# Two weight buffers in place of three, and one-hot tiles with two picks innermost

## What is computed

```
h = tok(x)                                   # embeddings, 3 graph vectors, projection, layernorm
h = h + conv(layernorm(h))                   # causal convolution along the sequence, generated filter
h = h + ffn(layernorm(h))                    # mixture of experts, 8 experts, top 2

def ffn(x):                                  # 8192 rows of 192
    logits = x @ Wr.T                        # (rows, 8)
    vals, idx = top_k(logits, 2)
    share = softmax(vals)
    e_out[e] = gelu(x @ Wi[e].T + bi[e]) @ Wo[e].T + bo[e]    # 192 -> 768 -> 192
    return sum_k share[k] * e_out[idx[k]]
```

## Time and profile before

| | |
|---|---|
| median of 3 runs | 1200.1 us (1199.15 to 1202.99) |
| the profiled execution | 1199.93 us, span 1198.0 us, mean granted clock of TensorE 0.784 |
| busy: PE, PEld, DVE | 955.7 (80%), 907.0 (76%), 615.1 us (51%) |
| busy: ACT, POOL | 518.6 (43%), 670.7 us (56%) |
| DMA | 146.96 MB, 123 GB/s in the mean |
| the costliest groups | L883 and L884 ACT gelu 212.4 and 214.6 us; L510 POOL scatter 236.6; L730 to L732 PE down 211.6, 209.9, 209.7; L711 to L715 PE up 116.6 each |

### The profile page before, as it was taken

How to read it: one execution, slowest core, us unless ns; L and a number is a source line. 1 busy time by engine, 2 the same in 40 slices (tenths; PEclk the granted TensorE clock), 3 DMA queues, 4 the chain that set the end, 5 groups by cost and what they waited for, 6 DMA issues and landing times. The chain is left out here.

```text
span 1198.0 us, 22895 instructions
## 1 busy us (share of the span) xinstructions
PE 955.7 (80%) x7666; PEld 907.0 (76%) x7666; DVE 615.1 (51%) x2089; ACT 518.6 (43%) x1211; POOL 670.7 (56%) x592
## 2 busy tenths in 40 slices
PE   1678677768677687594977699999988998999991
PEld 0578677778677687594964399999978998999981
DVE  2035343445444456538957356665544654665551
ACT  1002121311212123355755376767655665767660
POOL 6455564646565640003520268867767777888774
PEclk9975665656665666795555599999999999999996
DMA  6315261616162533581098174485486465434342
GB/s 208 106 53 176 81 209 53 217 50 214 46 222 94 170 110 114 167 241 53 1 256 263 28 199 62 61 224 129 86 218 151 60 141 120 61 61 61 61 51 30
DMA packets 101114, 146.96 MB, mean 123 GB/s; under 512 B 13476, under 2 KB 81223, under 8 KB 98983
## 3 DMA queue, kind: packets, MB, share of 16 engines
q0 software_dynamic: 39552, 53.26, 23.0%
q1 hardware_dynamic: 60470, 82.26, 21.8%
q10 hardware_dynamic: 1008, 10.34, 2.4%
HBM read 107.00 MB, written 38.82 MB: 122 GB/s over the span
## 5 line engine op out<-in xcount | busy, mean ns | idle before, releaser
L883 ACT ACTIVATE Hs<-bank,U 128x256 bf16<-128x256 f32 x426 | 212.4, 498 | 182.6 <-PE bank L715 153.8
L474 POOL DMA_INDIRECT ev_g<-in_word_emb,ids_i x192 | 192.9, 1004 | 166.1 <-PE bank L573 111.9
L510 POOL DMA_INDIRECT out<-Hs,id_s x142 | 236.6, 1666 | 85.4 <-issue 83.3
L1204 DVE TENSOR_TENSOR Hs<-Hs 128x512 bf16<-128x512 f32 x213 | 147.5, 692 | 146.6 <-ACT Hs L884 131.3
L884 ACT ACTIVATE Hs<-bank,U 128x256 f32<-128x256 f32 x426 | 214.6, 504 | 0.0
L730 PE MATMUL bank<-U,Hs 128*128 128x192 bf16 x852 | 211.6, 248 | 0.2 <-issue 0.2
L732 PE MATMUL bank<-U,Hs 128*128 128x192 bf16 x852 | 209.9, 246 | 0.0
L731 PE MATMUL bank<-U,Hs 128*128 128x192 bf16 x852 | 209.7, 246 | 0.0
L501 POOL DMA_INDIRECT blob<-xtab_d,id_g x142 | 144.2, 1015 | 111.7 <-DVEq L1188 61.1
L573 PE MATMUL bank<-cs,ev_g 128*128 128x1 f32 x384 | 97.8, 318 | 42.6 <-issue 42.6
L572 PE MATMUL bank<-cs,ev_g 128*128 128x1 f32 x384 | 96.1, 314 | 39.4 <-issue 39.3
(11 more groups left out here) (183 smaller groups left out, 1735.2 us busy)
## 6 DMA issues: line engine op xcount, KB each, us to landing
U<-blob_d SPq DMA_DIRECT2D x20, 771.0 KB
U<-blob_d SPq DMA_DIRECT2D x20, 672.0 KB
adj_s<-in_adj SPq DMA_DIRECT2D x48, 256.0 KB
ev_g<-kpad_d SPq DMA_DIRECT2D x24, 512.0 KB, 5.3
wst<-in_wsrc SPq DMA_DIRECT2D x8, 1344.0 KB
blob_d<-blob ACTq DMA_DIRECT2D x7, 1443.0 KB
xtab_d<-U SPq DMA_DIRECT2D x4, 1552.0 KB, 8.8
out<-Hs SPq DMA_DIRECT2D x4, 1536.0 KB, 11.5
```

What stands on the lines that cost most here:

```text
L474: pool.indirect_dma_start(ev_g[:, p, j, b, :], None, t["word_emb"], bass.IndirectOffsetOnAxis(ap=ids_i[:, 1 + j, i * Q + b:i * Q + b + 1], ...
L510: pool.indirect_dma_start(out, bass.IndirectOffsetOnAxis(ap=id_s[:, 2 * q + h:2 * q + h + 1], axis=0), yo[:, q % RX, h, :], None, compute_ ...
L883: f(hh[w][:, d, :], ps, ACT.Gelu, bias=bi[:, d:d + 1])
L1204: last = v.tensor_tensor(hl[w][:, c:c + 2, :], hf[w][:, c:c + 2, :], hh[w][:, c:c + 2, :], ALU.subtract)
```

## The change

The weights get WB = 2 buffers, so even tiles use one and odd tiles the other; the other buffers stay at three. The one-hot tiles are laid out `(a m n i)`, with i = 2 picks innermost and m = 4 pairs outside the columns: PE reads a plane with a step of 2 elements, ACT's half of a tile is contiguous, and `iota_r` holds each number twice and is read four times over.

```diff
 W3 = 3
-ROUNDS = -(-NT // W3)
+WB = 2
+ROUNDS = -(-NT // WB)
...
-        iota_r = sb("iota_r", [128, NC, PICKS], bf16)
+        iota_r = sb("iota_r", [128, NC, 2], bf16)
...
-        hot_p = wst[:, 0:1024].bitcast(bf16).rearrange("p (a n i) -> p a n i", a=2, i=PICKS)
+        hot_p = wst[:, 0:1024].bitcast(bf16).rearrange("p (a m n i) -> p a m n i", a=2, m=PICKS // 2, i=2)
...
-        wbuf = [U_room[:, w * BLOB:(w + 1) * BLOB] for w in range(W3)]
+        wbuf = [U_room[:, w * BLOB:(w + 1) * BLOB] for w in range(WB)]
...
             def reload(it):
-                for w in range(W3):
-                    q = W3 * it + w
+                for w in range(WB):
+                    q = WB * it + w
                     if isinstance(q, int) and q >= NT:
                         break
-                    e, held = expert(q), expert(q - W3)
-                    sp.wait_ge(gelu, FC // 2 * (q - W3 + 1))
+                    e, held = expert(q), expert(q - WB)
+                    sp.wait_ge(gelu, FC // 2 * (q - WB + 1))
...
-                    sp.wait_ge(biased, q - W3 + 1)
+                    sp.wait_ge(biased, q - WB + 1)
...
-                    last = mm(sums(i % TB), hot_p[:, g % 2, :, i], hot_s[:, g % 2, :, i], start=False, stop=False)
+                    last = mm(sums(i % TB), hot_p[:, g % 2, i // 2, :, i % 2], hot_s[:, g % 2, i // 2, :, i % 2], start=False, stop=False)
...
             def up_tile(q):
-                it, w = q // W3, q % W3
+                it, w = q // WB, q % WB
...
-                x0, x1, x2 = (xgT[:, w, c, :] for c in range(3))
+                x0, x1, x2 = (xgT[:, q % W3, c, :] for c in range(3))
...
-                    i = slice(k * TB, (k + 1) * TB)
-                    last = f(hot_s[:, g % 2, :, i], hot_q[:, g % 2, :, i], ACT.Copy, scale=powers[:, k, g:g + 1])
+                    m = slice(k * TB // 2, (k + 1) * TB // 2)
+                    last = f(hot_s[:, g % 2, m, :, :], hot_q[:, g % 2, m, :, :], ACT.Copy, scale=powers[:, k, g:g + 1])
...
-                here = places[:, g, :, :].rearrange("p k t -> p (k t)")
-                return v.tensor_tensor(out, iota_r[:, 0:width, :], repeat(here, 1, width), ALU.is_equal)
+                here = places[:, g, :, :].rearrange("p k (m i) -> p (k m) i", i=2)
+                return v.tensor_tensor(out, repeat(iota_r[:, 0:width, :], 1, PICKS // 2), repeat(here, 2, width), ALU.is_equal)
```

More of the change, by code:

```diff
@@ L215, in tower @@
         seg = wst[:, 1600:1600 + E * B].rearrange("p (e b) -> p e b", e=E)
-        hot_p = wst[:, 0:1024].bitcast(bf16).rearrange("p (a n i) -> p a n i", a=2, i=PICKS)
-        hot_q = old_adj[:, 0:NC * PICKS].bitcast(bf16).rearrange("p (a n i) -> p a n i", a=2, i=PICKS)
-        hot_s = old_adj[:, NC * PICKS:2 * NC * PICKS].bitcast(bf16).rearrange("p (a n i) -> p a n i", a=2, i=PICKS)
+        hot_p = wst[:, 0:1024].bitcast(bf16).rearrange("p (a m n i) -> p a m n i", a=2, m=PICKS // 2, i=2)
+        hot_q = old_adj[:, 0:NC * PICKS].bitcast(bf16).rearrange("p (a m n i) -> p a m n i", a=2, m=PICKS // 2, i=2)
+        hot_s = old_adj[:, NC * PICKS:2 * NC * PICKS].bitcast(bf16).rearrange("p (a m n i) -> p a m n i", a=2, m=PICKS // 2, i=2)
         def sums(i):
             return bank[5 + i // 2][:, (i % 2) * NC:(i % 2 + 1) * NC]
-        wbuf = [U_room[:, w * BLOB:(w + 1) * BLOB] for w in range(W3)]
+        wbuf = [U_room[:, w * BLOB:(w + 1) * BLOB] for w in range(WB)]
         flat = Hs[:, :, :].rearrange("p b d -> p (b d)")
@@ L303, in tower @@
         ids_done = sem("ids_done")
-        wi_in = [sem(f"wi_in{w}") for w in range(W3)]
-        wo_in = [sem(f"wo_in{w}") for w in range(W3)]
+        wi_in = [sem(f"wi_in{w}") for w in range(WB)]
+        wo_in = [sem(f"wo_in{w}") for w in range(WB)]
         xg_in = [sem(f"xg_in{x}") for x in range(RX)]
@@ L719, in down_tile @@
             def down_tile(q):
-                it, w = q // W3, q % W3
-                hi, lo = parts(wbuf[w])[3:5]
-                pe.wait_ge(wo_in[w], 16 * (it + 1))
+                it, w = q // WB, q % W3
+                hi, lo = parts(wbuf[q % WB])[3:5]
+                pe.wait_ge(wo_in[q % WB], 16 * (it + 1))
                 pe.wait_ge(hid, q + 1)
@@ L876, in hidden @@
             def hidden(q, w):
-                bi = parts(wbuf[w])[2]
+                bi = parts(wbuf[q % WB])[2]
                 for c in range(0, FC, 2):
@@ L901, in _ @@
             v.tensor_copy(iota_f[:, :], cst[:, 256:512])
-            v.tensor_copy(iota_r[:, :, :], repeat(cst[:, 256:256 + NC], 2, PICKS))
+            v.tensor_copy(iota_r[:, :, :], repeat(cst[:, 256:256 + NC], 2, 2))
             v.memset(ones_b[:, :], 1.0)
@@ L1161, in _ @@
                 after(dve, hot_s_ready, g - 1)
-                one_hot(hot_q[:, g % 2, :, :], slq, g, NC).then_inc(hot_q_ready, 1)
+                one_hot(hot_q[:, g % 2, :, :, :], slq, g, NC).then_inc(hot_q_ready, 1)
                 after(dve, pick_used, g - 1)
-                one_hot(hot_p[:, g % 2, :, :], slp, g, 128).then_inc(hot_p_ready, 1)
+                one_hot(hot_p[:, g % 2, :, :, :], slp, g, 128).then_inc(hot_p_ready, 1)
                 if g == 1:
@@ L1213, in bias_out @@
                 v.tensor_tensor(yo[:, x, :, :], bank[5 + w][:, 0:2 * D].rearrange("p (h d) -> p h d", h=2),
-                                repeat(parts(wbuf[w])[5], 1, 2), ALU.add).then_inc(biased, 1)
+                                repeat(parts(wbuf[q % WB])[5], 1, 2), ALU.add).then_inc(biased, 1)
                 fence()
```

## The result

The changed kernel took 1181.14 us in the median of 4 runs (1176.67 to 1193.08), the kernel before 1199.65 on the same chip (1199.15 to 1202.99): a ratio of 0.985, interval 0.981 to 0.989. The profiled execution took 1180.91 us, span 1178.8. The forecast was 1185.6, range 1179 to 1199. Two later comparisons of the same kernel on other chips gave 0.992 (0.988 to 0.995) and 0.985 (0.982 to 0.987).

What follows compares the result with a forecast made beforehand. The prediction took the table, then GpSimd's chain of scatters, to bound the kernel. Its terms -9.0 (table), -0.3 (start), -6 (loads) and +1 (tile 3) summed to -14.3, from 1199.9 to 1185.6 us, range 1179 to 1199.

Steps and rivals of the forecast that it cites:

- The table: One-hot table stage: PE's matmuls start every 0.118 us instead of 0.26 at the smaller step; -9.0 us (0 to -10.2).
- the loop over two buffers: In the table: scalings, eight matmuls and two semaphores take 2.95 us for two groups, setting 1.47 us a group.
- Fewer loads: Expert stage: two buffers reload fewer tiles at expert changes, so scatters wait less; -6 us (0 to -8).
- a hidden seventh: Expert stage: a possible further change of expert beside the six read from the trace; 14 or 15 up-loads expected.
- +1: Tile 3, start of the expert stage: GpSimd waits for PE there, so the later load costs 1 us.
- Later loads: Expert stage: up-loads wait for tile q-2; PE waits 2.5 us a change, hidden under GpSimd's lag; 0 (to 16).
- Rival 1: Expert stage: loads later still, PE becomes the bound from 3.7 us of waits a change; 1212 us, chance 0.12.
- 3 and 29 "less 6": Expert stage: GpSimd's lag (3) and own delays (29, less 6) together hide 26 us of PE's waits.
- The start: DVE's first pass: the `iota_r` cast shrinks by about 0.5 us of 0.74; -0.3 us (0 to -0.5).

Runs made afterwards that it cites:

- the table alone: Changed kernel with three weight buffers as before, keeping only the new one-hot layout; ratio 0.997 (0.994 to 1.000) to the kernel before.
- three reloads: Changed kernel, two buffers, but a tile reloads whenever its expert differs from that of three tiles before; 1198.1 us, ratio 0.998 to the kernel before.
- early up-load: Changed kernel, but SP issues the next tile's up-load ahead of the current tile's down-load; ratio 0.988 (0.983 to 0.993) to the kernel before.
- long cast in place: Changed kernel with `iota_r` at its old 1136 elements and old cast, one-hots reading two of each eight; ratio 0.996 to the kernel before.
- buffers alone: Kernel before with two weight buffers and the old one-hot layout; ratio 0.995 (0.992 to 0.998) to the kernel before.
- weight side at the old step: Changed kernel, but PE's stationary one-hot (positions) keeps eight picks innermost, the moving one has two; one execution, table 23.69 us.
- four picks innermost: Changed kernel with four picks innermost in place of two, so PE reads at a step of 8 bytes; one execution, table 24.12 us.
- long cast aside: Changed kernel with the old 1136-element cast into a separate tile, short `iota_r` copied from it later; ratio 0.985 (0.983 to 0.988) to the kernel before.
- one pick innermost: Changed kernel with one pick innermost in place of two, each plane contiguous; one execution, table 38.45 us.
- SyncE slower: Changed kernel with four more reads of an expert's number ahead of each up-load; 1094.7 us against 1082.1 of the changed kernel there.

## Why the prediction was right

**The table** (-9.0): right in mechanism and nearly in size. 0.118 us a matmul was forecast and 0.113 to 0.119 measured, ACT came next as worked out, and the table shrank by 9.8 us in every profile with the changed layout as it is. A group takes ACT's own 1.40 us (4.20 for three groups) and not 1.47: the loop over two buffers, with 0.25 us for two semaphores that no row shows, wasn't the bound. The kernels with other steps tell why: it is the moving operand, with one element in 16 bytes. That the whole 9.8 us reach the end isn't shown by times: the table alone brought 0.2 to 7.6.

**Fewer loads** (-6): 14 up-loads, as the count of changes without a hidden seventh. In the three bursts the waits of scatters over 0.30 us are 14.3 us (7.05, 5.05, 2.16) for 10 tiles, 1.4 each, in place of 23.4 for 14. The forecast took 5 to 7 us off, 9.1 went. But in the second profile of the same kernel these waits are 20.9 us, no shorter in the body than with three buffers. The stage is what counts. Its profiles, in us, without those of the three reloads and the early up-load above; "late" are PE's waits on up-loads, "at 0.50" is the time at the lower clock between the first and the last tiles, "for DVE" is what GpSimd waits ahead of gathers:

| kernel, chip | loads | stage | late | at 0.50 | for DVE |
|---|---|---|---|---|---|
| before | 20 | 522.4 | 0 | 7 | 9.1 |
| the table alone, A | 20 | 522.7 | 0 | 7 | 10.8 |
| changed, the result | 14 | 514.2 | 14.5 | 0 | 12.2 |
| changed, B | 14 | 525.0 | 14.7 | 14 | 14.0 |
| long cast in place, B | 14 | 515.9 | 16.0 | 0 | 12.8 |
| buffers alone, A | 14 | 519.5 | 18.0 | 7 | 26.3 |
| weight side at the old step, B | 14 | 524.8 | 18.4 | 17 | 33.4 |
| four picks innermost, B | 14 | 524.0 | 19.2 | 10 | 29.9 |
| changed, C | 14 | 509.1 | 11.0 | 0 | 15.4 |
| long cast aside, C | 14 | 512.9 | 11.4 | 0 | 12.8 |
| one pick innermost, C | 14 | 512.3 | 12.1 | 3 | 20.8 |
| SyncE slower, C | 14 | 524.8 | 20.8 | 17 | 26.9 |

Apart from SyncE slower, all kernels with 14 loads in this table have the same expert stage. Away from chip C it takes 514 to 525 us, with three buffers 522 to 523. So no profile shows the gain for sure. The times do: the buffers alone bring 5.5 us (1.8 to 9.2) and the long cast in place 4.9 (0.6 to 9.1), which holds the forecast's 5 (-6 and +1). That the result's own profile has 8.2 us is in part luck.

**Later loads** (0): the size of the waits was right (2.5 a change forecast; 14.5 us over six changes, 2.4 each). That they cost nothing was right for the profiled execution of the result: behind tile 15 GpSimd never waits 0.5 us or more for DVE there. It wasn't right for every execution. In the weight side's and the four picks' profiles, with the same expert stage, PE's waits are 18 to 19 us, the clock falls, GpSimd waits 30 to 33 us for DVE, and the stage is 524 to 525. The prediction made the later loads too cheap in two ways. Rival 1 put the point from which PE decides at 26 us of waits; with 20.8 (SyncE slower) the stage had grown by 15.7 us, and with 18.0 (buffers alone) GpSimd had lost its lag in part of the stage. The term that was mis-sized is GpSimd's lag and its own delays there, 3 and 29 "less 6": the lag of 15 us at the end of the kernel before is built up by late scatters, and when these are fewer the cover is less. And a wait was priced at its length, without what the clock loses around it.

**The start** (-0.3): this is the step that isn't settled. In all seven profiles with a short cast that aren't from chip C the first matmul of the column means comes at 43 to 48 us; with the old layout at 34.3 and 34.9, and with the changed layout and the long cast in place at 39.5. The cast itself shrank from 0.74 to 0.29 us, as forecast. By the last column-means matmul, 440.9 after and 443.0 before, nothing is left of it, and over all these profiles that point lies anywhere from 436 to 455. So its price at the end can't be read from profiles. The runs leave room for one: the table alone brought 3.8 us (0.2 to 7.6) where its own table was 9.8 us shorter, and on chip C, without the shift, the whole change brought 16.9 (14.2 to 19.7), more than the 10.0 (5.7 to 14.2) on chip B. That fits a loss of some us at the start on A and B; it isn't shown.

**The sum**: 14.3 forecast. Measured 18.2 (13.6 to 23.0), 10.0 (5.7 to 14.2) and 16.9 us (14.2 to 19.7) in three comparisons. The forecast lies among them, the mechanism of the table is shown, and that of the stage holds in some executions and not in others. The spread between the comparisons, 8 us, is larger than the whole term of the stage, and the halves alone brought 3.8 and 5.5, 9.3 together. So that the sum came so near is in part luck.

## What to carry to other kernels

Before trusting that a plane of an interleaved tile is free to read, look at how many elements of it lie in 16 bytes: for PE's moving operand one costs a factor of 2.2, two (a step of 8 bytes) a tenth, and with four (a step of 4 bytes) nothing is lost. When choosing the layout take the engines together: two innermost is enough for DVE's pairs, one isn't. A wait that is hidden by another engine's lag stays hidden only as long as the lag, and an edit that cures the lag takes the cover away too: size the two together, and test the cover by making the wait longer, not only by taking it away. When PE begins to wait, read the granted clock around the waits too: it can cost as much again.

## What the runs showed of the hardware that I had not expected

**DVE and a row pitch of 16 bytes.** Pairs of bf16 read contiguous: 0.74 us for 1136 elements. Pairs of bf16 every 16 bytes: 1.14 us, unlike both the paired rate and the unpaired 1.32. The Trainium skill (Vector Engine (DVE) Microarchitecture Reference, section 5.1) puts the condition on the innermost dimension only; the 1.32 us with one element innermost agrees with it, the 1.14 isn't foreseen by it.

**DVE's small instructions beside GpSimd's gathers.** The same kernel at the same place of its start, DVE in the order of time, in the profile of the result's section and on chip C:

```profile
21.96 0.21 DVE L927 TENSOR_SCALAR ys<-ys 16x128 f32<-16x128 f32 x1
22.26 0.21 DVE L929 TENSOR_SCALAR ys<-ys 16x128 f32<-16x128 f32 x1
23.57 0.28 DVE L935 SCALAR_TENSOR_TENSOR ys<-ys 16x128 f32<-16x128 f32 x1 [1.10 <-issue]
24.27 0.28 DVE L935 SCALAR_TENSOR_TENSOR ys<-ys 16x128 f32<-16x128 f32 x1 [0.42 <-issue]
```
```profile
16.42 0.47 DVE L927 TENSOR_SCALAR ys<-ys 16x128 f32<-16x128 f32 x1
16.96 0.21 DVE L929 TENSOR_SCALAR ys<-ys 16x128 f32<-16x128 f32 x1
17.26 0.99 DVE L935 SCALAR_TENSOR_TENSOR ys<-ys 16x128 f32<-16x128 f32 x3
```

In the first DVE sits idle for 0.4 to 1.1 us between such instructions (and for 1.9 us ahead of a memset shortly before), on chip C these run back to back, while GpSimd issues a gather every 1.25 us in both. The Trainium skill (SBUF — State Buffer, section "Who interferes with whom") tells of a port pair that DVE and GpSimd share and that whoever issues first holds; I would expect such a lock to show in both, and it shows in one. So the cause stays open.

**Chips differ in a part of the kernel.** On chip C the kernel before takes 1098.5 us. In the changed kernel's profile there the last matmul of the column means is at 345.3 us in place of 440.9, and the table is as long as elsewhere (23.43), the stage nearly so (509.1 against 514.2). The part with the small gathers is some 95 us shorter, with the same instructions. Ratios on one chip can be compared; times across chips can't.
